# A graph network on one core: scale and bias in one operation per block, a masked copy and a root in another order, and a copy on another engine

## The reference

```
norm = deg_inv_sqrt[row] * deg_inv_sqrt[col] * edge_weight
xw   = einsum('ni,tio->tno', x, W)                # four types
out  = segment_sum(xw[edge_type, col] * norm, row) + b
z    = leaky_relu(out, 0.01)                      # z1, z2, z3
x    = layernorm(x + (x + z1 + z2 + z3) / 4)      # (x - mean) / sqrt(var + 1e-5)
```

## Time and profile before

| | before |
|---|---|
| median of three runs | 8947.23 us (8946.75 to 8949.12) |
| profiled execution | 8944.74 us |
| its span | 8942.5 us |
| PE busy | 5975.2 us, 67% |
| VectorE (DVE) busy | 5414.9 us, 61% |
| ScalarE (ACT) busy | 2172.1 us, 24% |
| POOL busy | 6393.3 us, 71% |
| mean granted clock of PE | 0.619 |
| chain: POOL L733 | 33% of the span |

### The profile page before, as it was taken

How to read it: one execution, slowest core, us unless ns; L and a number is a source line. 1 busy time by engine, 2 the same in 40 slices (tenths; PEclk the granted TensorE clock), 3 DMA queues, 4 the chain that set the end, 5 groups by cost and what they waited for, 6 DMA issues and landing times.

```text
span 8942.5 us, 151268 instructions
## 1 busy us (share of the span) xinstructions
PE 5975.2 (67%) x30961; PEld 4629.3 (52%) x30962; DVE 5414.9 (61%) x15776; ACT 2172.1 (24%) x6655; POOL 6393.3 (71%) x6521
## 2 busy tenths in 40 slices
PE   4886565656666565655657565665656878888886
PEld 4664444444444444444444444444444777777776
DVE  9996444444445444444445444444446888888888
ACT  6550000000001000000001000000003888888887
POOL 0667777777776777777776777777775777777775
PEclk9995555555556555555556555555555887888887
DMA  1002122212224222212123222222222444444443
GB/s 51 35 35 56 53 53 53 53 53 53 53 63 97 53 53 53 53 53 53 53 53 103 53 53 53 53 53 53 53 53 68 115 116 114 116 115 115 115 115 98
DMA packets 432687, 612.45 MB, mean 68 GB/s; under 512 B 232038, under 2 KB 249491, under 8 KB 432539
## 3 DMA queue, kind: packets, MB, share of 16 engines
q0 software_dynamic: 208832, 428.96, 19.0%
q1 hardware_dynamic: 223707, 182.02, 6.5%
HBM read 437.29 MB, written 51.28 MB: 55 GB/s over the span
## 4 chain that ended last, share of the span: by engine, by line
POOL 42%; issue 32%; DMA 9%; DVE 7%; PE 6%; ACT 2%; POOLq 1%; DVEq 1%; SPq 0%; ACTq 0%
POOL g_rows L733 33%; POOL a_roll L758 9%; DMA g_rows<-gcn_table,rec_idx 7%; ACT a_cand L899 2%; DMA a_rows<-a_roll 1%; POOLq L754 1%; PE bank L1161 1%; DVE lo_hot L1227 1%; DVE v_hot L1352 1%; PE wide L1161 1%; PE wide L1044 1%; PE wide L1122 1%; PE wide L1179 0%; DMA a_roll<-gat_table,src_plane 0%; DVE p_hot L1227 0%
## 5 line engine op out<-in xcount | busy, mean ns | idle before, releaser
L733 POOL DMA_INDIRECT g_rows<-gcn_table,rec_idx x4743 | 4487.0, 946 | 1445.8 <-issue 1358.9
L1161 PE MATMUL bank<-g_rows,g_hot 128*128 x7440 | 1906.6, 437 | 1097.5 <-POOLq L710 1037.8
L1161 PEld LDWEIGHTS bank<-g_rows,g_hot 128*128 128x128 f32 x7440 | 1638.5, 324 | 1552.5 <-issue 1550.7
L1604 DVE TENSOR_TENSOR acc<-acc,bank 128x512 f32 x930 | 639.6, 688 | 2092.9 <-PE bank L1161 2090.1
L1589 DVE TENSOR_SCALAR g_hot<-bank,rec_lo,rec_w 128x128 f32<-128x128 f32 x5580 | 1897.3, 402 | 2.2 <-DVE mv L1647 2.0
L758 POOL DMA_INDIRECT a_roll<-gat_table,src_plane x1612 | 1521.2, 944 | 494.6 <-issue 470.0
L1161 PE MATMUL wide<-g_rows,g_hot 128*128 x3720 | 952.4, 437 | 598.0 <-POOLq L710 579.7
L1161 PEld LDWEIGHTS wide<-g_rows,g_hot 128*128 128x128 f32 x3720 | 818.5, 323 | 826.1 <-issue 824.8
L899 ACT ACTIVATE a_cand<-a_miss,a_rows 128x128 f32<-128x128 bf16 x3608 | 1100.2, 387 | 302.2 <-DMA a_rows<-a_roll 299.2
L862 ACT ACTIVATE rows<-bank,inv_deg 128x512 f32<-128x512 f32 x34 | 23.4, 688 | 3914.9 <-PE bank L1122 3914.9
L1604 DVE TENSOR_TENSOR acc<-acc,wide 128x512 f32 x465 | 319.8, 688 | 1063.5 <-PE wide L1161 1062.6
(11 more groups left out here) (268 smaller groups left out, 5604.7 us busy)
## 6 DMA issues: line engine op xcount, KB each, us to landing
a_rows<-a_roll SPq DMA_DIRECT2D x451, 264.0 KB
g_rows<-gcn_table,rec_idx POOLq DMA_INDIRECT x4743
gcn_table<-rows SPq DMA_DIRECT2D x147, 256.0 KB
a_roll<-gat_table,src_plane POOLq DMA_INDIRECT x1612
e_dst<-by_dst_dst SPq DMA_DIRECT2D x451, 2.0 KB
gat_table<-acc SPq DMA_DIRECT2D x7, 462.0 KB
out_x<-xs SPq DMA_DIRECT2D x6, 448.0 KB
gcn_slots<-nothing SPq DMA_DIRECT2D x4, 468.0 KB, 6.8
```

Of the source, the lines that this page charges most:

```text
L733: pool.indirect_dma_start(out=g_rows[:, tile % RING, :], out_offset=None, in_=gcn_tables[layer % 2], in_offset=bass.IndirectOffsetOnAxis(a ...
L1161: last = nc.tensor.matmul(sums_of(j)[:, bass.ds(place, D)], g_hot[:, j % 3, k, :], g_rows[:, bass.ds(slot, 1), :].rearrange("p g d -> p (g ...
L1604: V.tensor_tensor(dst_ap, dst_ap, sums_of(j).rearrange("p (k d) -> p k d", k=GP), ALU.add).then_inc(s_gadd, 1)
```

## The change

`next_z` makes z of a block in one operation, times `inv_deg` (one value per partition) plus bias, so four operations of 128 columns stand where two of 512 stood. In layer 2 `masked(n - 1)` is issued behind `next_z(n)` where it was ahead of it. `ln_stats` no longer adds the constant; `ln_sqrt` gets it as the bias of its root, from a new tile `eps` with two columns, and in layer 2 the root stands ahead of the copy of the transposed blocks in ScalarE's order. In layers 0 and 1 the copy of the transposed blocks is ScalarE's, behind the rows of the batch before, and no longer VectorE's. The signal `s_ln` comes from the last aggregate itself.

```diff
--- before.py
+++ after.py
@@ -206,6 +206,7 @@
         bias = sb("bias", [P, 4, D])
         att = sb("att", [P, 2, D])
         inv_deg = sb("inv_deg", [P, NB])
+        eps = sb("eps", [P, 2])
         deg_mask = sb("deg_mask", [P, NB])
         falls_i = sb("falls_i", [1, 1], I32)
         gcn_at = sb("gcn_at", [33, ALL_GROUPS, GP + 1], I32)
@@ -843,10 +844,10 @@
             act.wait_ge(s_rec, 2 * CH)
             act.wait_ge(s_count, 9)
 
-            def ln_sqrt(n, blocks):
+            def ln_sqrt(n, blocks, constant):
                 cs = slice(blocks.start, blocks.stop)
                 act.wait_ge(s_ln, n + 1)
-                nc.scalar.sqrt(mv[:, cs, 1], mv[:, cs, 1]).then_inc(s_ln2, 1)
+                nc.scalar.activation(mv[:, cs, 1], mv[:, cs, 1], ACT.Sqrt, bias=constant).then_inc(s_ln2, 1)
 
             def gat_rows(n):
                 for b in BATCHES[n]:
@@ -865,12 +866,16 @@
                 for n in range(NBATCH + 1):
                     if n >= 1 and layer < 2:
                         rows_of(n - 1)
+                    if n < NBATCH and layer < 2:
+                        act.wait_ge(s_tT, turns(layer + 1, n) + 1)
+                        nc.scalar.copy(*turned(n)).then_inc(s_tc, 1)
+                    if n < NBATCH and layer == 2:
+                        ln_sqrt(n, BATCHES[n], eps[:, 0:1])
                     if n >= 1 and layer == 2:
                         act.wait_ge(s_tT, turns(3, n - 1) + 1)
                         nc.scalar.copy(*turned(n - 1)).then_inc(s_tc, 1)
                         gat_rows(n - 1)
                     if n < NBATCH and layer == 2:
-                        ln_sqrt(n, BATCHES[n])
                         act.wait_ge(s_third, n + 1)
                         for b in BATCHES[n]:
                             last = nc.scalar.activation(xs[:, b, :], xs[:, b, :], ACT.Identity,
@@ -921,7 +926,7 @@
                 last.then_inc(s_divided, 1)
             for c in range(len(CHUNKS) + 1):
                 if c < len(CHUNKS):
-                    ln_sqrt(NBATCH + c, CHUNKS[c])
+                    ln_sqrt(NBATCH + c, CHUNKS[c], eps[:, 1:2])
                 if c >= 1:
                     act.wait_ge(s_den, 1 + c)
                     for b in range((c - 1) * C, min(c * C, NB - DVE_LAST)):
@@ -1213,6 +1218,8 @@
             V.memset(pads[0][:, :], PAD_NODE)
             V.memset(pads[1][:, :], float(PAD_NODE)).then_inc(s_fill, 1)
             V.memset(dst_next[:, :], PAD_NODE).then_inc(s_fill, 1)
+            V.memset(eps[:, 0:1], 16.0 * 1e-5)
+            V.memset(eps[:, 1:2], 1e-5)
             V.memset(zeros[:, :], 0.0).then_inc(s_fill, 1)
 
             def pairs(ap, shape):
@@ -1603,19 +1610,18 @@
                         dve.wait_ge(s_gadd, q.at(0, 1, adds + 1))
                         V.tensor_tensor(dst_ap, dst_ap, sums_of(j).rearrange("p (k d) -> p k d", k=GP), ALU.add
                                         ).then_inc(s_gadd, 1)
+                        if 0 <= n < NBATCH:
+                            dve.wait_ge(s_gadd, q.at(0, 1, adds + 2))
+                            next_z(layer, slice(BATCHES[n].start, BATCHES[n].stop))
                         if layer == 2 and 1 <= n <= NBATCH:
                             masked(n - 1)
                         if 0 <= n < NBATCH:
-                            dve.wait_ge(s_gadd, q.at(0, 1, adds + 2))
-                            next_z(layer, slice(BATCHES[n].start, BATCHES[n].stop))
                             if layer < 2:
-                                dve.wait_ge(s_tT, turns(layer + 1, n) + 1)
-                                V.tensor_copy(*turned(n)).then_inc(s_tc, 1)
                                 if n == NBATCH - 1:
                                     chain(V.scalar_tensor_tensor(xs[:, :, :], xs[:, :, :], 1.0 if layer else 5.0,
                                                                  z[:, :, :], ALU.mult, ALU.add))
                             else:
-                                ln_stats(BATCHES[n], 16.0 * 1e-5)
+                                ln_stats(BATCHES[n])
                                 hot(q)
                                 third(n)
                 run_steps(dve, GRP, 3, 2, body, NBATCH + 1)
@@ -1623,29 +1629,25 @@
 
             def next_z(layer, bs):
 
-                shape = [P, bs.stop - bs.start, D]
-                chain(V.tensor_tensor(z[:, bs, :], acc[:, bs, 0:D],
-                                      spread(inv_deg[:, bs].unsqueeze(2), shape), ALU.mult))
-                chain(V.tensor_tensor(z[:, bs, :], z[:, bs, :],
-                                      spread(bias[:, layer, :].unsqueeze(1), shape), ALU.add))
+                for b in range(bs.start, bs.stop):
+                    last = V.scalar_tensor_tensor(z[:, b, :], acc[:, b, 0:D], inv_deg[:, b:b + 1],
+                                                  bias[:, layer, :], ALU.mult, ALU.add)
+                chain(last)
                 chain(V.scalar_tensor_tensor(z[:, bs, :], z[:, bs, :], 0.01, z[:, bs, :],
                                              ALU.mult, ALU.max))
                 if layer < 2:
-                    dve.sem_inc(s_z[layer + 1], shape[1])
+                    dve.sem_inc(s_z[layer + 1], bs.stop - bs.start)
                 else:
                     chain(V.tensor_tensor(xs[:, bs, :], xs[:, bs, :], z[:, bs, :], ALU.add))
 
-            def ln_stats(blocks, eps):
+            def ln_stats(blocks):
 
                 for b in blocks:
                     last = V.bn_stats(stats[:, b, :], xs[:, b, :])
                 chain(last)
                 for b in blocks:
                     last = V.bn_aggr(mv[:, b, :], stats[:, b, :])
-                chain(last)
-                var = mv[:, blocks.start:blocks.stop, 1]
-                chain(V.tensor_scalar(var, var, eps, None, ALU.add))
-                dve.sem_inc(s_ln, 1)
+                last.then_inc(s_ln, 1)
 
             def masked(n):
 
@@ -1750,7 +1752,7 @@
                     quotients(slice(0, NB - C))
                     dve.sem_inc(s_den, 1)
                     divide(CHUNKS[0])
-                    ln_stats(range(C), 1e-5)
+                    ln_stats(range(C))
 
                 def add(h):
                     hs = slice(h * (HC + 1), (h + 1) * (HC + 1))
@@ -1802,7 +1804,7 @@
                         chain(V.tensor_tensor(xs_v, xs_v, acc_v[:, cs, :, 0:HC], ALU.add))
                     else:
                         divide(cs)
-                    ln_stats(range(cs.start, cs.stop), 1e-5)
+                    ln_stats(range(cs.start, cs.stop))
                 cs = CHUNKS[c - 1]
                 dve.wait_ge(s_ln2, NBATCH + c)
                 chain(V.reciprocal(mv[:, cs, 1], mv[:, cs, 1]))
```

## The result

The changed kernel takes 8965.67 us (median of 16 runs, 8963.47 to 8971.33), the kernel before 8948.01 us in the same rounds (8946.37 to 8950.14). The ratio is 1.002, with a 95% interval of 1.0013 to 1.0027: **17.7 us slower**, just under the 17.9 that the prediction calls 0.2%. The forecast was 8959.4.

The account below looks back on a forecast made before the run. Closed loops over PE and VectorE at the layer ends, not PE alone, were taken as the bound the change touches. Terms -9.3 + 24 - 2.5 = +12.2 us on 8947.23 gave 8959.4; range 8943 to 8969.

Parts of the forecast that it names:

- Masked behind the block update: End of layer 2: VectorE's z and xs steps come between add and masked; cycle 10.75 us against 8.73.
- The root first: End of layer 2, ScalarE: root queued ahead of the copy waits for statistics; 0.25 us late, cycle 11.0 us.
- The root's bias tile costs nothing: Root on ScalarE: the bias tile adds no time, since the root already had a constant's tile.
- z in one operation per block: VectorE, layer ends: four 128-wide operations cost 1.13 us against 1.45, saving 0.3 us per batch (0 to 0.5).
- The copy on ScalarE: Layers 0 and 1: barely hidden, done at 1.4 to 1.5 us; last batch 0.25 late; both layers -9.3 us.
- The failed step: Layers 0 and 1: PE's cycle falls from 5.54 to 5.15 us (5.0 to 5.35); both layers -9.3 us.
- The constant: Last normalisation: VectorE's addition and signal go, 0.35 us in each of seven steps, -2.5 us.
- is worth nothing: Layer 2: the constant's 0.35 us falls in VectorE's slack, no gain once masked is behind z.
- Rival 4: Layers 0 and 1: row copies hold ScalarE's copy or rows land late; cycle 5.4 to 5.5, 8965 to 8967; chance 0.13.
- Rival 1: Layers 0 and 1: PE is the bound, cycle stays near 5.5 us, no gain; 8969 us; chance 0.12.
- Rivals 2 and 3: 2: layer 2's order harmless, 8927, chance 0.05; 3: PE gets 2.4 GHz in layer 2's end, 8938, chance 0.05.

Follow-up runs that it names:

- Root_back: Changed kernel with layer 2's root again behind the rows of the batch before, masked still behind the block update; ratio to the kernel before 1.0005.
- Load_early: Changed kernel with PE's read of slot addresses moved ahead of the batch's last product in layers 0 and 1; ratio to the kernel before 1.0010.
- before_again: Kernel before, unchanged, traced again on the same slower chip as the variants; end of layer 2 119.3 us.
- after_again: Changed kernel, unchanged, run again on a later, slower chip; ratio to the kernel before 1.0007 (0.9993 to 1.0021).
- only_root_constant: Kernel before with one edit: the root takes the variance's constant, VectorE's addition and its signal are gone; ratio 1.0000 (0.9987 to 1.0012).

## Why the prediction was right, and where it was not

The sign held, and so did the account of the loss, which comes from the end of layer 2. The range held by 3.3 us (8965.67 against a top of 8969), although one of the three terms was off by 7.5. The 17.7 us are 5.5 more than the forecast +12.2. By its own steps:

- **Masked behind the block update.** Forecast: a cycle of 10.75 without the root's part. Root_back has 10.79, and PE's part of 6.75 is 6.74 in it (masked ends at 8749.97, the next add starts at 8756.71). Right.
- **The root first.** Forecast 0.25 late, measured 0.38 (11.17 - 10.79). The root starts 1.47 us behind masked's end instead of 1.35, and that 0.12 is nearly all of the miss: the copy behind it starts 0.20 after the root (6790.78, 6790.98), as the forecast had it. "The root's bias tile costs nothing" was wrong as a duration: the root takes 0.30 us where it took 0.21. The copy starts ahead of the end that the profile shows for the root, so whether those 0.09 us cost the round anything stays open. Both terms together: +24 forecast, +25.4 measured.
- **z in one operation per block.** Forecast 1.13, measured 1.15, 0.262 apart. The gain of 0.3 us shows in the first round of layers 0 and 1 (6.14 to 5.86; the clock hides it in the second) and, in before's order of layer 2, with 0.27 a round. The Trainium skill's errata formula ("VectorE: DVE Perf Modes", "The TRN2 errata") had given an estimated 1.16 for the four; the sum agrees with the trace, though the operations are not alike: a lone one takes 0.35 us, and four in a row start every 0.262.
- **The copy on ScalarE.** It is hidden, as forecast: it ends 1.37 us behind the transposes (2712.97 + 0.58 against 2712.18) and the products begin at 1.84. In the last batch of layer 0, where nothing hides it, products start 1.41 us behind the transposes (2733.85, 2735.26); the forecast had 1.6, and before had 1.39, so the 0.25 that it charged there did not come. Of the time that VectorE gains PE can use only 0.07 us a round.
- **The failed step** is the cycle of PE: "part of it runs ahead, so I take 5.15 (between 5.0 ... and 5.35)". Measured 5.47. The two ends were wrong in different ways. 5.0 lies under the floor of 5.28, and so does the 5.15. And the 5.35 of the earlier trace rows was read as a cycle with the slot arithmetic in it that would only get shorter; it is one round, the last; the changed kernel's last rounds are 5.38 and 5.42, and its others reach 5.62. What holds the arithmetic back is not VectorE's signal but the read ahead of it in PE's own instruction order, which waits in line behind the last product. Worth 11 x 0.32 = 3.5 us a layer; the term came to -1.8 instead of -9.3. The rule that I weighed, the queue of the Trainium skill's "TensorE: Matmul & The Clock Gate" ("Architectural detail: the array is 16× 32×32, not 1× 128×128"), says that weight loads are pulled ahead of matmuls; that register reads and arithmetic would be hidden with them was my step. Load_early is the cycle with everything early, and it is 5.28.
- **The constant.** Forecast 0.35 in each of seven steps, measured 0.44 to 0.48 (reciprocals 4.09 us apart before, 3.63 after), 2.8 in all. The forecast took the idle time behind the aggregates' shown end. But the addition needed the aggregates and started 0.03 us behind that end (8932.53), while the reciprocal that now follows needs nothing of them and starts 0.09 us ahead of it (8941.91 against 8942.00). The sentence that it "is worth nothing" in layer 2 stands untried for the order it was written for. In before's order masked waits 0.69 to 0.76 us for ScalarE's block in seven rounds of twelve, and that block waits for VectorE's statistics: the constant lies on that path and gains 0.47 a round, 5.2 us over the end (104.92 in before_again, 99.72).
- **Rivals.** Rival 4's time (8965 to 8967) and round (5.4 to 5.5) came out, its cause did not: neither row copies nor ScalarE's copy held PE. Rival 1, which put PE at the bound, is the nearer mechanism: it asked for distances above 5.5, and they average 5.47, with single ones up to 5.62. It was weighed at 0.12, and what it lacked was the reason, the read. Rivals 2 and 3 fell with the 11.17: the clock in the end of layer 2 was 0.54, as argued.

The terms as measured, -1.8 + 25.4 - 2.8, give +20.8; the medians give 17.7, with an interval of 11.6 to 24.2 (0.0013 and 0.0027 of 8948). The 3 us between them are inside that interval.

## What to carry to other kernels

Before work is moved in a queue, write down the ring that it lies in: which engine waits for it, and what that engine could do meanwhile. Taking a wait of 0.7 us from VectorE put its 2.6 us of z work in line with PE's 6.75, and the round grew by 2.4. Two orders that close the same ring hide each other, so undo both before one is called harmless. When an engine is no longer waiting for another, count its own instructions one by one, register reads included, before giving its cycle a number.

## What the runs showed of the hardware that was not expected

**The clock rose at different moments of the same code.** PE's clock in slices of 1 us at the end of layer 0, in the first trace of the changed kernel and in after_again:

```profile
2676.00:2677.00 1.00, 1.00 (x3) 0.48 (x2) 0.96 (x3) 0.69 (x1) 0.71 (x1) 0.50 0.24 66
2677.00:2678.00 1.00, 1.00 (x3) 0.39 (x3) 0.84 (x4) 0.33 (x1) 0.94 (x1) 0.84 0.48 150
2678.00:2679.00 1.00, 1.00 (x4) 0.43 (x3) 0.67 (x3) 0.83 (x2) 0.73 (x1) 1.00 0.73 236
```

```profile
3434.00:3435.00 1.00, 1.00 (x2) 0.00 (x0) 0.96 (x3) 0.00 (x0) 0.00 (x0) 0.50 0.00 0
3435.00:3436.00 1.00, 0.45 (x1) 0.00 (x0) 0.96 (x4) 0.51 (x1) 0.00 (x0) 0.66 0.00 0
3436.00:3437.00 1.00, 0.41 (x4) 0.41 (x4) 0.84 (x3) 0.17 (x1) 0.00 (x0) 1.00 0.00 0
```

PE was busy at 1.2 GHz ahead of the rise in both. The same code reached 2.4 GHz some 12 us behind its first transposes (2664.90) in the one and 5 us behind (3430.73) in the other. The second round takes 8.43 or 5.42 us by it. These are different chips, but the chip alone does not decide it: before_again was run to see whether the moment repeats, and it did, to 0.1 us (5.55 and 7.12 against 5.54 and 7.04), while only_root_constant, on the same chip and with before's code in layers 0 and 1, has 8.53 and 5.55. In the five traces with the changed kernel's code in these layers the two rounds together take 10.9 to 15.5 us. So a single trace can show 3 us at a layer end that no edit made; the +2.9 of the first table is of that size, and what decides the moment was not tried.

**PE's sequencer pauses on a slower chip.** In the gather loop of layer 1 POOL waits for PE, which it did for 0.3 us on the first chip (before_again, then before):

```profile
POOL g_rows L733 <- PE bank L1161: 452.6, 59, 38.2
...
POOL g_rows L733 <- PE wide L1161: 216.7, 35, 17.9
```

```profile
POOL g_rows L733 <- PE wide L1161: 0.3, 1, 0.3
```

PE itself waits for no engine there: its matmuls at 4004.52 and 4008.01 stand behind 5.08 and 2.72 us of "issue". Single register operations of its sequencer (L1157, L1158) take 0.70 and 0.71 us in that stretch (4000 to 4012 us), where the same operations otherwise take 0.04. The kernel takes 37 to 40% longer on the slower chips; whether these pauses are all of it, and what makes them, was not tried. In the three layer ends of before_again, on whose like the readings here rest, no operation of L1158 takes more than 0.04 us.
